# Rounding the feed-forward weights during the first attention instead of during the feed-forward layer

## The reference

```python
def _quantized_matmul(x, w, scale):
    wq = w.astype(jnp.float8_e4m3fn).astype(x.dtype)
    y = jnp.einsum('bsi,io->bso', x, wq)
    return y * scale
gate = jax.nn.silu(_quantized_matmul(x, gate_w, gate_scale))
up = _quantized_matmul(x, up_w, up_scale)
return _quantized_matmul(gate * up, down_w, down_scale)
```

## Time and profile before

| | |
|---|---|
| median of three runs | 2400.84 us |
| the profiled execution, its own time | 2404.99 us |
| its span in the trace | 2402.8 us |
| TensorE matmul, busy | 2179.4 us, 91% |
| VectorE, busy | 1595.1 us, 66% |
| ScalarE, busy | 1208.3 us, 50% |
| GpSimd, busy | 594.5 us, 25% |
| DMA, mean over the span | 81 GB/s |

### The profile page before, as it was taken

The page is one execution under the profiler, slowest core; times in us unless marked ns, Lnnn a source line. Parts: engine busy times, 40 slices in busy tenths (PEclk is TensorE's granted clock), DMA queues, the critical chain, the costliest instruction groups (busy, mean ns, idle before and its releaser), DMA issues. The chain is left out here.

```text
span 2402.8 us, 38656 instructions
## 1 busy us (share of the span) xinstructions
PE 2179.4 (91%) x12367; PEld 1888.2 (79%) x12367; DVE 1595.1 (66%) x3802; ACT 1208.3 (50%) x3284; POOL 594.5 (25%) x1194
## 2 busy tenths in 40 slices
PE   4999999999997679996999999999999998479993
PEld 4898998898886457775788888888888887268882
DVE  5777777777777992225466666666666666667776
ACT  3445555455553312223566666666666664247772
POOL 1010000000000462222333323343333321025441
PEclk8999999999999899998899999999999998779997
DMA  6112112121110220001112111111112110258886
GB/s 240 50 61 74 61 49 74 61 74 48 61 62 1 81 82 1 0 0 35 53 45 73 58 44 52 47 66 44 52 44 74 49 36 1 74 213 290 289 277 260
DMA packets 74346, 195.51 MB, mean 81 GB/s; under 512 B 8432, under 2 KB 39176, under 8 KB 61472
## 3 DMA queue, kind: packets, MB, share of 16 engines
q1 hardware_dynamic: 64416, 173.60, 20.5%
q0 software_dynamic: 7680, 16.80, 2.1%
q10 hardware_dynamic: 2176, 4.19, 0.5%
HBM read 177.78 MB, written 25.17 MB: 84 GB/s over the span
## 5 line engine op out<-in xcount | busy, mean ns | idle before, releaser
L502 PE MATMUL bank<-l_wkv_hi,l_ctxT 128*128 128x256 f32 (+1 forms) x1024 | 280.4, 346 | 9.5 <-PEq L135 9.0
L791 DVE TENSOR_TENSOR l_v_lo<-bank,l_v_hi 128x128 fp32r<-128x128 f32 (+1 forms) x256 | 91.6, 358 | 223.4 <-ACT l_v_hi L688 222.1
L791 DVE TENSOR_TENSOR l_pT_lo<-bank,l_pT_hi 128x512 fp32r<-128x512 f32 x256 | 175.1, 684 | 81.7 <-ACT l_pT_hi L713 81.7
L502 PE MATMUL bank<-l_wo_hi,l_oT_hi 128*128 128x512 f32 x528 | 217.7, 412 | 2.8 <-DVE l_oT_lo L791 2.8
L707 ACT ACTIVATE l_probs<-l_scored,l_nbias 128x256 f32<-128x256 f32 x256 | 128.2, 501 | 166.6 <-DVE l_nbias L844 163.2
L502 PE MATMUL bank<-xnT_hi,l_wq_hi 128*128 128x512 f32 x512 | 210.4, 411 | 0.0
L502 PE MATMUL bank<-l_wo_lo,l_oT_hi 128*128 128x512 f32 x528 | 209.2, 396 | 0.0
L502 PEld LDWEIGHTS bank<-l_wkv_hi,l_ctxT 128*128 128x128 f32 x1024 | 184.3, 194 | 30.9 <-issue 9.4
L502 PE MATMUL bank<-l_wo_hi,l_oT_lo 128*128 128x512 f32 x528 | 208.3, 394 | 0.0
L502 PE MATMUL bank<-xnT_hi,l_wq_lo 128*128 128x512 f32 x512 | 203.3, 397 | 0.0
L502 PE MATMUL bank<-xnT_lo,l_wq_hi 128*128 128x512 f32 x512 | 202.5, 395 | 0.0
(11 more groups left out here) (254 smaller groups left out, 5973.0 us busy)
## 6 DMA issues: line engine op xcount, KB each, us to landing
l_ctxT<-ctx_split SPq DMA_DIRECT2D x64, 1024.0 KB, 4.8
moe_raw_gu<-in_L_ffn_gate_up_proj SPq DMA_DIRECT2D x32, 1024.0 KB
moe_raw_dn<-in_L_ffn_down_proj SPq DMA_DIRECT2D x32, 512.0 KB
l_raw_a<-in_L_xattn_Wq SPq DMA_DIRECT2D x16, 512.0 KB, 5.7
l_raw_a<-in_L_xattn_Wo SPq DMA_DIRECT2D x16, 512.0 KB, 5.3
x_sb<-in_x SPq DMA_DIRECT2D x4, 1024.0 KB, 11.4
ctx_split<-ct SPq DMA_DIRECT2D x4, 1024.0 KB, 11.1
xn_rows<-xn SPq DMA_DIRECT2D x16, 256.0 KB, 2.4
```

Of the source, the lines that this page charges most:

```text
L502: mm = nc.tensor.matmul(out, a[x], b[y], start=(i == 0), stop=(i == n - 1))
L791: nc.vector.tensor_tensor(pair[1], src, pair[0].bitcast(F32), ALU.subtract).then_inc(done, 1)
```

## The change

A new helper, rounding, works beside attention l0. In each hg it takes an eighth of each of the three matrices as one piece of 128x768 (i = 0 gate, 1 up, 2 down): SyncE loads the three raw pieces, VectorE masks the exponents of piece g at the end of its iterations g = 0, 1, 2, GpSimd then does the three other steps (maximum and multiply, add, subtract) at the end of its own iteration g, and SyncE stores the piece to a DRAM scratch in iteration g+1. The layer norm ahead of the feed-forward layer then starts 36 loads that bring all rounded weights from the scratch into ffn_w; the feed-forward stage has no rounding left, and its products wait for four groups of three slices. The two attention stages now share one set of semaphores, which SyncE clears in the feed-forward stage.

```diff
@@ -259,7 +260,7 @@
     a.wkv_flat = [w[:, :, :].rearrange("p k n -> p (k n)") for w in a.wkv]
     a.raw_b_flat = a.raw_b[:, :, :].rearrange("p k n -> p (k n)")
     a.wq_in, a.wkv_in, a.ctx_in, a.w_hi, a.wq_split, a.wkv_split = (
-        k.sem(f"{name}_{n}") for n in ("wq_in", "wkv_in", "ctx_in", "w_hi", "wq_split", "wkv_split"))
+        k.layer_sem(n) for n in ("wq_in", "wkv_in", "ctx_in", "w_hi", "wq_split", "wkv_split"))
     wq_v = Wq.rearrange("(k p) n -> p k n", p=P)
     wk_v = Wk.rearrange("(k p) n -> p k n", p=P)
     wv_v = Wv.rearrange("(k p) n -> p k n", p=P)
...
         def sem(n):
-            return k.sem(f"{name}_{n}")
+            return k.layer_sem(n)
         wo = pair("wo", [P, HB, D])
...
@@ -399,6 +400,8 @@
                 sp.dma_start(gain_in[:, 1:2], gk.rearrange("(p a) -> p a", a=1)).then_inc(const_in, 16)
             else:
                 sp.dma_start(mask_u8[:, :], mask.rearrange("(a b) s -> a (b s)", a=1).broadcast_to([P, T])).then_inc(const_in, 16)
+            if side is not None:
+                side.sync_start(sp)
             sp.wait_ge(kv_made, TG)
             load_ctx(sp, 1)
@@ -415,8 +418,12 @@
                     if g == 1 and not over(hg + 1, 0):
                         sp.wait_ge(wo_split, hg + 2)
                         load_wq(sp, hg + 1)
+                    if side is not None:
+                        side.sync(sp, hg, g, over(hg + 1, 0))
             iterations(sp, iteration)
+            if side is not None:
+                side.sync_end(sp)
...
@@ -488,6 +495,8 @@
                     if g == 2 and not over(hg + 1, 0):
                         weights_lo(wq_of[0], raw_wq_of[0], hg * 4 + 5, wq_split)
                         weights_lo(wkv_flat, raw_b_flat, hg * 4 + 6, wkv_split)
+                    if side is not None:
+                        side.gpsimd(pool, hg, g)
             iterations(pool, iteration)
@@ -949,6 +958,8 @@
                     split_q(hg, g, 1)
                     if rms:
                         biases(hg, g + 1, 0)
+                    if side is not None:
+                        side.vector(dve, hg, g)
             iterations(dve, iteration)
...
+def rounding(k, st, gate_w, up_w, down_w):
+    nc = k.nc
+    r = Parts()
+    cols = NF * D // NHG
+    wide = F // NHG
+    raw = [st.enter_context(nc.sbuf_tensor(f"round_raw{i}", [P, cols], F32)) for i in range(3)]
+    magic = st.enter_context(nc.sbuf_tensor("round_magic", [P, cols], F32))
+    rounded = st.enter_context(nc.sbuf_tensor("round_out", [P, cols], F32))
+    raw_in = [k.sem(f"round_raw_in{i}") for i in range(3)]
+    masked, chain, done, stored = (k.sem(f"round_{n}") for n in ("masked", "chain", "done", "stored"))
+    r.gate, r.up = (nc.dram_tensor(f"round_{n}", (D, F), F32, kind="Internal").ap() for n in ("gate", "up"))
+    r.down = nc.dram_tensor("round_down", (F, D), F32, kind="Internal").ap()
+    def piece(i, hg, source):
+        if i < 2:
+            w = ((gate_w, up_w) if source else (r.gate, r.up))[i]
+            return w.rearrange("(k p) f -> p k f", p=P)[:, :, bass.ds(hg * wide, wide)]
+        w = down_w if source else r.down
+        return w.rearrange("(f p) n -> p f n", p=P)[:, :, bass.ds(hg * (D // NHG), D // NHG)]
+    def tile(i, t):
+        return t[:, :].rearrange("p (k f) -> p k f", k=KD if i < 2 else NF)
+    def load(sp, hg):
+        for i in range(3):
+            sp.dma_start(tile(i, raw[i]), piece(i, hg, True)).then_inc(raw_in[i], 16)
+    def store(sp, hg, i):
+        sp.wait_ge(done, hg * 3 + (i + 1))
+        sp.dma_start(piece(i, hg, False), tile(i, rounded)).then_inc(stored, 16)
+    def round_off(pool, hg, i):
+        def step(ins, n):
+            ins.then_inc(chain, 1)
+            pool.wait_ge(chain, hg * 6 + (2 * i + n))
+        pool.wait_ge(masked, hg * 3 + (i + 1))
+        apart(k, pool)
+        step(nc.gpsimd.tensor_scalar(magic[:, :], magic[:, :], 2.0 ** -6, 1.5 * 2.0 ** 20, ALU.max, ALU.mult), 1)
+        step(nc.gpsimd.tensor_tensor(raw[i][:, :], raw[i][:, :], magic[:, :], ALU.add), 2)
+        if i > 0 or not isinstance(hg, int) or hg > 0:
+            pool.wait_ge(stored, hg * 48 + 16 * i)
+        nc.gpsimd.tensor_tensor(rounded[:, :], raw[i][:, :], magic[:, :], ALU.subtract).then_inc(done, 1)
+    def mask(dve, hg, i):
+        dve.wait_ge(raw_in[i], hg * 16 + 16)
+        if i > 0 or not isinstance(hg, int) or hg > 0:
+            dve.wait_ge(done, hg * 3 + i)
+        apart(k, dve)
+        nc.vector.tensor_scalar(magic[:, :].bitcast(U32), raw[i][:, :].bitcast(U32), 0x7F800000, None, ALU.bitwise_and).then_inc(masked, 1)
+    def sync_start(sp):
+        load(sp, 0)
+    def sync(sp, hg, g, last):
+        if g >= 1:
+            store(sp, hg, g - 1)
+        if g == NG - 1 and not last:
+            load(sp, hg + 1)
+    def sync_end(sp):
+        sp.wait_ge(stored, 48 * NHG)
+    def gpsimd(pool, hg, g):
+        if g < 3:
+            round_off(pool, hg, g)
+    def vector(dve, hg, g):
+        if g < 3:
+            mask(dve, hg, g)
+    r.sync_start, r.sync, r.sync_end, r.gpsimd, r.vector = sync_start, sync, sync_end, gpsimd, vector
+    return r
...
     def load(sp, f):
-        at = bass.ds(f * P, P)
-        r0 = a.raw[0][:, :].rearrange("p (k f) -> p k f", f=P)
-        sp.dma_start(r0[:, 0:KD, :], gate_v[:, :, at]).then_inc(a.raw_in[0], 16)
-        sp.dma_start(r0[:, KD:half // P, :], up_v[:, 0:2, at]).then_inc(a.raw_in[0], 16)
-        yield
-        r1 = a.raw[1][:, 0:2 * P].rearrange("p (k f) -> p k f", f=P)
-        sp.dma_start(r1, up_v[:, 2:4, at]).then_inc(a.raw_in[1], 16)
-        sp.dma_start(a.raw[1][:, 2 * P:half], down_v[:, bass.ds(f, 1), :]).then_inc(a.raw_in[1], 16)
-        yield
+        at = slice(P * f, P * (f + 1))
+        row = a.w[:, f, :].bitcast(F32)
+        w_in = a.w_in[f // W_GROUP]
+        sp.dma_start(row[:, 0:D].rearrange("p (k f) -> p k f", f=P), gate_v[:, :, at]).then_inc(w_in, 16)
+        sp.dma_start(row[:, D:2 * D].rearrange("p (k f) -> p k f", f=P), up_v[:, :, at]).then_inc(w_in, 16)
+        sp.dma_start(row[:, 2 * D:3 * D], down_v[:, f, :]).then_inc(w_in, 16)
     def sync(sp):
-        for _ in load(sp, 0):
-            pass
         sp.dma_start(a.scale_rows[0:NF, :], gate_scale.rearrange("(f p) -> f p", p=P)).then_inc(a.scales_in, 16)
         sp.dma_start(a.scale_rows[NF:2 * NF, :], up_scale.rearrange("(f p) -> f p", p=P)).then_inc(a.scales_in, 16)
         sp.dma_start(a.dsc[:, :], down_scale.rearrange("(a n) -> a n", a=1).broadcast_to([P, D])).then_inc(a.scales_in, 16)
-
-    a.load, a.sync, a.scalar, a.gpsimd = load, sync, lambda act: None, lambda pool: None
+        for f in range(NF):
+            load(sp, f)
+    a.sync, a.scalar, a.gpsimd = sync, lambda act: None, lambda pool: None
     return a
...
-        w = sb("w", [P, NF, 3 * D], F32R)
-        magic = [sb(f"magic{i}", [P, half]) for i in range(2)]
-        raised = [sb(f"raised{i}", [P, half]) for i in range(2)]
         silu = [sb(f"silu{i}", [P, GT]) for i in range(2)]
         fuse = [sb(f"fuse{i}", [P, GT]) for i in range(2)]
         fz = [[sb(f"fz{i}_{p}", [P, GT], F32R) for p in ("hi", "lo")] for i in range(2)]
         scales = sb("scales", [P, 2 * NF])
-        ysc = [r[:, 0:D] for r in raised]
+        ysc = [sb(f"ysc{i}", [P, D])[:, :] for i in range(2)]
         block = st.enter_context(nc.Block())
...
         @block.sync
         def _(sp):
-            with sp.Fori(0, NF - 1) as f:
-                steps = start.load(sp, f + 1)
-                for c in range(2):
-                    sp.wait_ge(magic_made, f * 2 + (c + 1))
-                    next(steps)
+            for s in k.layer_sems.values():
+                sp.sem_clear(s)
         def groups(eng, body):
...
         @block.gpsimd
         def _(pool):
-            def round_off(f):
-
-                for c in range(2):
-                    pool.wait_ge(magic_made, 2 * f + c + 1)
-                    nc.gpsimd.tensor_tensor(w[:, f, half * c:half * (c + 1)], raised[c][:, :], magic[c][:, :], ALU.subtract).then_inc(w_ready, 1)
-
             def body(i, add):
                 for f in range(NF):
-                    if i is None and f + 1 < NF:
-                        round_off(f + 1)
                     pool.wait_ge(fz_hi, level(i, add, NF, f + 1))
                     nc.gpsimd.tensor_tensor(fz[f % 2][1][:, :], fuse[f % 2][:, :], fz[f % 2][0][:, :].bitcast(F32),
                                             ALU.subtract).then_inc(fz_split, 1)
-            round_off(0)
             groups(pool, body)
...
         @block.vector
         def _(dve):
-
-            def round_up(f):
-
-                for c in range(2):
-                    dve.wait_ge(raw_in[c], 32 * (f + 1))
-                    if f >= 1:
-                        dve.wait_ge(w_ready, 2 * (f - 1) + c + 1)
-                    nc.vector.tensor_scalar(magic[c][:, :].bitcast(U32), raw[c][:, :].bitcast(U32), 0x7F800000, None,
```

(25 more changed lines are left out.)

15 lines of the change are left out of this document (5 added, 10 removed).

## The result

The changed kernel takes **2434.84 us** in the median of four runs (2433.85 to 2435.74), against 2400.45 us for the kernel before beside it. The ratio is 1.0144, with a 95% interval of 1.0126 to 1.0161: 34.4 us slower. The prediction said 2407 us and a range of 2374 to 2430, so it was wrong, by 28 us. The profiled execution took 2435.22 us, its span is 2433.5 us.

The account below looks back on a forecast made before the run. TensorE was taken to bound attention l0, VectorE's rounding the first feed-forward group. The median 2400.84 less 35.4 gained in the feed-forward layer plus 41.2 lost in the attention gave 2406.6, say 2407 us; range 2374 to 2430.

Parts of the forecast that it names:

- what the feed-forward layer gains: Feed-forward layer: first product 5.3 us earlier, first silu of group 0 to group 1 30.1 us less; together 35.4 us.
- the mechanism of the loss, and its place: Attention l0: running GpSimd operations hold VectorE's l_nbias, clamp and scalings, so TensorE waits before weigh_v; 41.2 us lost.
- I take 0.78, nearest to the fill, since one operand passes: GpSimd's maximum and multiply on 768 columns: assumed 0.78 us, between 0.72 from a fill and 1.85 for two inputs.
- Rival (b): GpSimd's first operation is as slow as a two-input one: 66.8 us lost in attention l0, 2432 us; chance 0.13.
- that every running GpSimd operation holds its partner until it ends: Attention l0: l_nbias, clamp, scalings and mask wait for the running GpSimd operation's end; part of the 41.2 us lost.
- one hold for a pair of scalings: Attention l0, g=2 to 3: query weights' low part holds the scaling to 227.38; 2.37 us late, 1.85 lost.
- 4.4 us for the last pair, less than for the others: Attention l0: the last pair, with no query weights to split, loses 4.4 us, the seven others 5.25 each.
- Stalls of 1 to 3 us should not bring the clock down: Attention l0: TensorE keeps its full clock through such waits, as it did with 29% idle; no cost added.
- I cost the loads at nothing: Layer norm before the feed-forward layer: 36 weight loads on SyncE land before their use; 0 us.
- stores, raw loads and masks are nearly free: Attention l0: stores and raw loads cost nothing; a mask of 0.56 us delays what follows by 0.48 on VectorE.
- Rival (a): Attention l0: the holds are absorbed, 0.36 us per piece, 8.6 in all; 2374 us; chance 0.17.
- (c): Feed-forward layer: weights come late at half the load rate, the last group waits 22 us; 2429 us; chance 0.05.

Follow-up runs that it names:

- experiment 10: The kernel before, rounding still in the feed-forward layer: GpSimd does maximum and multiply, VectorE mask, add and subtract, the scales' copy behind the first masks; 2423.95 us.
- experiment 3: The changed kernel without GpSimd's maximum and multiply; only add and subtract stay on GpSimd; 2407.34 us.
- experiments 2: The changed kernel with only GpSimd's maximum and multiply; add and subtract are left out; 2382.72 us.
- experiment 6: The changed kernel with GpSimd's add and subtract first and the maximum and multiply last, its result unused; 2416.09 us.
- experiment 5: The changed kernel with GpSimd's steps on piece 2 moved from the end of g=2 to the end of g=3; 2418.12 us.
- experiment 4: The changed kernel with only the first three slices' weight loads issued in the layer norm, the rest in the feed-forward block; 2427.16 us.
- experiment 1: The changed kernel without GpSimd's three rounding operations, raw weights stored; masks, loads and stores stay; 2376.91 us.
- experiment 8: The changed kernel with all four steps of a piece on VectorE, in a row where the mask stood; 2453.66 us.

## Why the prediction was wrong

- **Right: what the feed-forward layer gains.** 5.3 us at the start as forecast; from silu to silu 64.35 us for the 64.0 worked out. In all, 35.0 for 35.4. The shift shrinks by 4 us more behind group 1 (34.8 to 30.7), but that is no gain of the change: from the first silu of group 1 to the end of the span pass 1497.3 us in the profile of before, 1493.2 in that of the changed kernel, and 1492.8 in that of experiment 10, which has before's code there. The execution profiled for before was slow in that stretch.
- **Right: the mechanism of the loss, and its place.** Two-input GpSimd operations hold the clamp and the scalings to their end, the reciprocal goes free, and weigh_v waits for split_p. The durations of the two-input steps, 1.84 and 1.83 for 1.85, were right. TensorE stood at 94.5 of 100 us, forecast 94, but that agreement is luck: a loss of 7.5 us in a pair of some 95 is 8%, and stretches at 1.2 GHz count as busy.
- **Wrong step, the largest: "I take 0.78, nearest to the fill, since one operand passes".** The one-input step takes 2.78 us, outside even my bounds of 0.72 to 1.85. A fill reads nothing, and a row that reads nothing bounds no operation that does arithmetic. Rival (b), in which this step is slow, gave 2432 us, close to what was measured, but for a part of the reason only: it had the step at 1.85, itself holding VectorE throughout, and the loads at nothing. With the two-input steps alone (experiment 3) the attention grows by 32.6 us, so the forecast's 41.2 was not short of what the rest costs; the slow step is what it lacked.
- **Wrong step: that every running GpSimd operation holds its partner until it ends.** The one-input step does so only near its start and its end (an l_nbias that starts 0.52 us into its 2.77 is back after 0.32). It costs 6 to 9 us by itself (experiments 2 and 6). Its larger price is that it delays the holds of the others, at g=2 to g=3 from l_nbias and a wait onto the clamp and both scalings, 18.7 us by experiment 6.
- **Wrong step: one hold for a pair of scalings.** I let the low part of the query weights or the subtract hold one instruction. In the timeline both scalings of a pair were held, one after the other by two GpSimd operations (3.14 us). Together with the late start this makes TensorE 3.6 us late at g=2 to g=3 before the clock is counted, where I had 1.85.
- **Wrong step: 4.4 us for the last pair, less than for the others.** It cost 9.2. I took away the hold by the query weights and kept the rest of a middle pair's walk, its slack too; in the last group there was none, as TensorE waited 2.72 us in before already, and 7.06 after.
- **Wrong step: "Stalls of 1 to 3 us should not bring the clock down".** In each of seven pairs a wait of about 2.8 us was followed by some 3 us at 1.2 GHz. At 1.07 us for each, this is some 8 of the 62 us. Between 130 and 760 us, experiment 5, whose longest wait is 1.67 us, has no drop, and experiment 6, with waits of up to 2.0, has two.
- **Wrong step: "I cost the loads at nothing", as SyncE "has nothing else".** True of the data, which came in time, and false of the block: it ends when SyncE has issued the last load. 7.6 us, shown by experiment 4.
- **Right: stores, raw loads and masks are nearly free.** 2.7 us in all (experiment 1). Rival (a), the holds absorbed, and (c), late weights, did not occur.

The sum with the measured terms: 2400.5 - 35.0 + 62.2 + 7.6 = 2435.3, beside 2434.8 measured. It leaves out the 4.1 us behind group 1, as they are of the single execution profiled for before, which ran 4.5 us above the median of 2400.45.

## What to carry to other kernels

An engine that looks free is not free for its neighbour: before moving work to GpSimd, walk through the neighbour's instructions in order and ask which would run beside a two-input operation, then take the work to where these are not links of the critical chain, or cut it into single steps and put them into the waits of the faster engine. Here the same twelve steps in a pair of heads cost attention l0, over all eight pairs, 76 us in blocks on VectorE, 62 with nine of them on GpSimd, and 1 us in VectorE's gaps. Look at the last turn of a loop by itself, too: slack read in a middle turn may be missing there. Issues of a long list of loads belong where their queue has time: a stage ends with the last list, also when that list only starts transfers.

## What the runs showed of the hardware that I had not expected

- GpSimd's maximum and multiply with two constants on 128x768 float32 takes 2.78 us and the maximum alone 2.13, both more than a two-input add of the same size (1.84); VectorE takes 0.56 for the first.
- GpSimd's maximum and multiply holds l_nbias, the clamp and the scalings until 0.84 us after its start and again from 2.0 us after its start to its end, and not between. In experiment 6 a pair of 128x256 scalings takes 1.0 us if it starts 0.23 after the step's start, and 0.62 if 1.08 after it; a clamp 0.36 after it takes 0.49. A two-input one holds them until it ends.
- SyncE's issue of a 256 KiB load takes 0.43 to 0.51 us for the first five. Once the DMA engines are full (363 GB/s) every third one, the last of a slice, takes 0.98 to 1.29 us, the others at most 0.63.
- TensorE's clock fell behind all seven waits of 2.84 us in the changed kernel between 130 and 760 us. In experiment 8 the wait of 2.92 us before project_kv came six times there and the clock fell behind three (290, 485 and 679 us), not behind the others (193, 387 and 582). In experiment 6 it fell behind two of seven waits of 1.9 to 2.0 us. What else decides was not settled.
